# Local attention of a windowed block: maxima over 8x7 queries with two heads side by side, key blocks of nine columns, outputs summed in two banks, band loads in rows of eight heads

## The chip, the cores and the metric

The kernel runs on one core of one Trainium2 chip. Times are device microseconds (us) of one execution; shorter is better. PE is the matmul engine TensorE (PEld its weight loads), DVE is VectorE, ACT ScalarE, POOL GpSimd, SP SyncE; SPq and ACTq are the queues through which SP and ACT issue transfers. SBUF is the on-chip memory of 128 partitions, PSUM the eight accumulator banks (`banks` in the rows).

## The reference, cut to what matters

Two images of 128 channels and 56x56 pixels go through a depthwise convolution, three attentions (over block means, over four selected blocks, over a 7x7 window), a gated sum, a convolutional MLP and a normalization. The change is in the window attention (8 heads of 16 channels, edge padding by 3):

```python
padded = jnp.pad(feat, ((0, 0), (3, 3), (3, 3), (0, 0)), mode='edge')
patches = jnp.stack([padded[:, dy:dy + 56, dx:dx + 56, :] for dy in range(7) for dx in range(7)], axis=3)
q = lin(Q, wq_w[2], wq_b[2]);  k = lin(patches, wk_w[2], wk_b[2]);  v = lin(patches, wv_w[2], wv_b[2])
attn = softmax(einsum('bnhd,bnwhd->bnhw', q, k) * 16 ** -0.5, axis=-1)
y_win = lin(einsum('bnhw,bnwhd->bnhd', attn, v), pj_w[2], pj_b[2])
y = g[..., 0:1] * y_cmp + g[..., 1:2] * y_sel + g[..., 2:3] * y_win + Q
```

## The kernel before, in words

The program has four stretches: convolution and small products (to about 98 us), projection of keys, queries and values of the window attention (`pjobs`, to about 232), the two small attentions (`c_body`, to about 382), the window attention (to about 712), then the MLP.

**Projection.** 42 jobs, 28 of keys and 14 of queries. PE projects (L629), ACT, DVE and POOL split each result into three bf16 parts whose sum is the f32 value (`pk`, a ring of four buffers), and SP stores all three with one DMA to `k_parts` or `q_parts` in DRAM (L370). ACT may refill a buffer only when its store has landed (L875).

**Window attention.** The work is cut in 14 jobs, one for each band of eight image rows of each image. A job's keys are a padded band of 14 rows and 62 columns, stored column by column (`KROWS` = 14). `K` and `Q` hold for each head 96 rows of products of parts (`TERMS`: six pairs of a query part and a key part, 16 rows each), then 30 rows of masks that add a huge negative number to every key outside a query's window, and 2 rows (`SHIFT0`) with the query's negated maximum. `load_band` brings a band two to three jobs ahead; ACT issues it in three groups, each one DMA of keys (L345, 1736-byte rows) and two of queries (L348, 896-byte rows).

A job has 16 steps (`STEPJ`), two for each of 8 strips of 7 columns (`SUBS`, 56 queries). In one step PE issues, in this order:
- A (L732): scores for the maxima of two heads, 112 queries (two strips) against 280 keys, 12 steps ahead of use (`LEAD`); DVE takes the maximum (L1264, `wn`);
- every fourth step S (L739): a transpose of the maxima, after DVE has split them in two bf16 parts (L1270, L1272); DVE copies it (L1277, `nT`) and SP moves it into the shift rows of `Q` (L403);
- scores (L751): keys as the stationary operand, 128 by 56 columns for each of 8 heads, into bank 4 or 5. ACT takes the exponential of the first 98 or 84 partitions (L929, `P`). The 13 key columns of a strip are taken as 7 and 6, one step each (`HCOLS`);
- products with the values (L766), two steps behind: for each head 17 output rows (16 channels and a row of ones, that gives the sum of the exponentials) in a quarter of the partitions, 56 columns, f32, which the trace shows as two passes. The two steps of a strip are summed in bank 6 or 7; ACT copies the strip to `OB` (L943).

After a job's last strip, SP moves the sums to `SR` (L419), DVE turns them into gated reciprocals in three bf16 parts (L1245 to L1255), SP spreads them (L426, `RB`), PE expands them (D, L776), DVE multiplies (L1282, `ON`), PE projects (Y, L782), DVE adds to `X` (L1292). A, S, D and Y share two slots of two PSUM banks in turn (`pa`, `slot_free`): each waits until DVE has read the slot that the second last of them wrote. SP also brings the values `Vw` for each strip and half (L414, 544-byte rows), from a ring of six.

The order on each engine is written out by the step number `q`. Engines wait on semaphores, and each engine runs its own list in order.

## Time and profile before

| | us |
|---|---|
| median of 3 runs (919.23 to 923.59) | 923.09 |
| span of the profiled execution | 922.4 |
| of it: first maxima to first scores of the window attention | 10.9 |
| first scores to last product with the values | 305.7 |
| from there to the last Y | 13.7 |
| PE busy over the whole span | 787.8 |
| DVE busy | 687.8 |
| ACT busy | 371.2 |

The profiled execution's own time is known only by its span. Busy times are unions: matmuls overlap in the array, so a step's cost on PE is read from the distance of two starts, not from the mean duration of an instruction. A line number is that of kernel.py before. PEclk is the granted clock of TensorE, 1.00 for 2.4 GHz and 0.50 for 1.2 GHz.

### The profile page before, as it was taken

The numbers are of one execution on the slowest core, as the hardware profiler recorded it, in microseconds if no ns is written. First come the engines' busy times: TensorE is split into PE (matmuls) and PEld (weight loads), VectorE is DVE, ScalarE is ACT, GpSimd is POOL, SyncE is SP. The second block draws the span as 40 slices with busy tenths as digits, with TensorE's granted clock in tenths as the row PEclk, the third lists the DMA queues.
The fourth block names the chain that finished last, engine by engine and source line by source line (L and its number), as shares of the span: only waits on it lengthen the run. The fifth ranks groups of instructions, "written<-read, shape, count | busy, mean of one in ns | idle before, by whom it ended". The sixth has DMA issues, their size and how long they took to land.

```text
span 922.4 us, 19487 instructions
## 1 busy us (share of the span) xinstructions
PE 787.8 (85%) x7573; PEld 452.1 (49%) x7573; DVE 687.8 (75%) x1442; ACT 371.2 (40%) x721; POOL 175.4 (19%) x236
## 2 busy tenths in 40 slices
PE   4958877776999999799888898888887999999993
PEld 2535433332344444366656666656664454455551
DVE  6976555665889999666777667677784988999971
ACT  2220334443333434134444444444455305445755
POOL 1100233332434444150000000000041034700000
PEclk9966888997689999857999888899999999999998
DMA  5000344554991000036676666677510000000000
GB/s 205 0 1 0 102 138 132 146 150 136 175 172 15 1 1 1 7 90 125 133 143 132 121 125 111 125 146 143 108 44 9 1 0 1 0 1 35 36 35 35
DMA packets 79504, 71.03 MB, mean 77 GB/s; under 512 B 10506, under 2 KB 77878, under 8 KB 78902
## 3 DMA queue, kind: packets, MB, share of 16 engines
q1 hardware_dynamic: 60934, 47.55, 21.4%
q10 hardware_dynamic: 18480, 22.24, 12.2%
q8 instruction: 60, 0.98, 0.5%
q14 instruction: 30, 0.25, 0.1%
HBM read 47.51 MB, written 21.57 MB: 75 GB/s over the span
## 4 chain that ended last, share of the span: by engine, by line
PE 38%; DVE 24%; issue 7%; ACT 4%; DMA 2%; ACTq 1%; SPq 1%; POOL 0%; DVEq 0%
PE banks L827 11%; DVE wn L1264 6%; PE banks L766 5%; PE banks L732 5%; PE banks L751 4%; DVE mx L1198 4%; DVE sm L1211 3%; PE banks L782 3%; DVE AC L1030 2%; DVE ON L1282 2%; DVE sm L1213 1%; DMA RB<-SB 1%; PE banks L716 1%; DVE SEB L1201 1%; ACTq L348 1%
## 5 line engine op out<-in xcount | busy, mean ns | idle before, releaser
L1264 DVE TENSOR_REDUCE wn<-banks 112x2 f32<-112x560 f32 x224 | 162.0, 737 | 53.6 <-PE banks L732 52.6
L929 ACT ACTIVATE P<-banks 98x448 f32<-98x448 f32 x224 | 120.0, 541 | 167.8 <-PE banks L751 133.6
L827 PE MATMUL banks<-FP,PTB 128*128 128x392 f32 x384 | 129.2, 493 | 1.0 <-DVE c L1295 0.9
L1030 DVE SCALAR_TENSOR_TENSOR AC<-XT,vec,AC 128x1540 f32<-128x1540 f32 (+5 forms) x48 | 115.1, 2401 | 1.1
L827 PEld LDWEIGHTS banks<-FP,PTB 128*128 128x128 f32 x384 | 72.8, 190 | 55.5 <-DVE c L1295 1.6
L766 PE MATMUL banks<-P,Vw 84*17 84x56 f32 (+1 forms) x3584 | 95.1, 227 | 2.1 <-issue 1.5
L479 POOL TENSOR_TENSOR SEB<-SEB,rg 112x392 f32<-112x392 f32 x112 | 58.3, 541 | 92.8 <-DVE rg L1218 92.8
L732 PE MATMUL banks<-K,Q 126*112 126x280 bf16 x288 | 71.1, 333 | 4.2 <-DVE wn L1264 3.7
L1127 DVE TENSOR_TENSOR pr<-pf,pk 128x434 f32<-128x434 f32 (+1 forms) x42 | 33.9, 807 | 51.1 <-ACT pk L884 50.3
L908 ACT ACTIVATE SEB<-SEB 112x424 f32<-112x424 f32 x56 | 31.2, 557 | 92.3 <-DVE SEB L1201 92.3
L463 POOL TENSOR_TENSOR pk<-pr,pk 128x434 bf16<-128x434 f32 (+1 forms) x42 | 42.7, 1018 | 127.9 <-DVE pk L1138 127.9
L766 PEld LDWEIGHTS banks<-P,Vw 84*17 84x17 f32 (+1 forms) x3584 | 55.9, 102 | 13.7 <-issue 2.8
L691 PE MATMUL banks<-PTB,VP 106*128 106x448 f32 x112 | 55.8, 587 | 4.8 <-ACT PTB L917 4.8
L751 PE MATMUL banks<-Q,K 128*128 128x56 bf16 x1152 | 56.9, 192 | 1.7 <-ACT P L929 1.7
L671 PE MATMUL banks<-Af,XT 128*112 128x424 f32 x112 | 56.0, 584 | 0.0
L751 PEld LDWEIGHTS banks<-Q,K 128*128 128x128 bf16 x1152 | 49.8, 100 | 9.8 <-issue 2.6
L514 POOL MEMSET FP<- 128x224 f32 x1 | 0.3, 284 | 268.4 <-PE banks L751 268.4
L553 PE MATMUL banks<-X,diag 128*128 128x440 f32 (+3 forms) x90 | 36.4, 569 | 12.6 <-ACT diag L847 12.6
L883 ACT ACTIVATE pf<-banks,vec 128x434 f32<-128x434 f32 x28 | 17.3, 617 | 70.2 <-PE banks L629 49.1
L1198 DVE TENSOR_REDUCE mx<-banks 112x8 f32<-112x392 f32 x112 | 37.1, 373 | 10.4 <-PE banks L672 10.3
L732 PE MATMUL banks<-FP 126*112 126x280 bf16 x160 | 38.7, 331 | 5.0 <-DVE wn L1264 3.2
L732 PEld LDWEIGHTS banks<-K,Q 126*112 126x112 bf16 x288 | 28.8, 140 | 25.5 <-DVE wn L1264 9.7
(225 smaller groups left out, 1294.1 us busy)
## 6 DMA issues: line engine op xcount, KB each, us to landing
k_parts<-pk SPq DMA_DIRECT2D x28, 325.5 KB, 4.0
K<-k_parts ACTq DMA_DIRECT2D x21, 434.0 KB, 5.1
Vw<-v_rows SPq DMA_DIRECT2D x112, 52.1 KB
FP<-k_parts ACTq DMA_DIRECT2D x12, 434.0 KB, 5.0
Vw<-v_rows SPq DMA_DIRECT2D x112, 44.6 KB
q_parts<-pk SPq DMA_DIRECT2D x14, 336.0 KB, 4.3
Q<-q_parts ACTq DMA_DIRECT2D x42, 112.0 KB, 5.3
v_rows<-vst SPq DMA_DIRECT2D x14, 263.5 KB
```

The lines of the kernel that those rows point to most:

```text
L463: g.tensor_tensor(p[:, SLOT[2], 0:cols], pr[n % 3][:, 0:cols], p[:, SLOT[1], 0:cols], ALU.subtract).then_inc(sem("parts_ready"), 1)
L479: g.tensor_tensor(dst, src, by, ALU.mult).then_inc(sem("c_norm"), 1)
L671: mm(s, XT[:, img, ds(t * BAND + c * TILE, TILE)], Af[img][:], start=True, stop=False)
L691: last = mm(bank(4 + img, C, BAND), VP[img][:, j, :], PT[img][:, j, :], start=(j == 0), stop=(j == PAIRS - 1))
L732: last = mm(PS[0:TILE, 2 * slot + e, 0:KROWS * TCOLS], Q[j % BUFS][0:SHIFT0, h, c * TILE:(c + 1) * TILE], K[j % BUFS][0:SHIFT0, h * KBAND ...
L751: last = mm(PS[:, 4 + q % 2, h * SUB:(h + 1) * SUB], K[j % BUFS][:, first:first + 128], Q[j % BUFS][:, h, c * SUB:(c + 1) * SUB], start=Tr ...
L766: last = mm(PS[QUAD * b:QUAD * b + VH, 6 + s % 2, u * SUB:(u + 1) * SUB], Vw[s % VRING][0:HKEYS[half], half, VH * h:VH * (h + 1)], P[p % 4 ...
L827: last = mm(bank(2 + place_in_unit, C, ZPIX), WT[:, dy, part, C * grp:C * (grp + 1)], D[:, part, QROWS * q + dy:QROWS * (q + 1) + dy, :].r ...
L929: a(P[q % 4][0:HKEYS[half], :], PS[0:HKEYS[half], 4 + q % 2, 0:HEADS * SUB], ACT.Exp).then_inc(sem("w_exp"), 1)
L1030: return ve.scalar_tensor_tensor(out=o, in0=src(ro + dy, rn, co + dx, cn), scalar=v(wcol + t), in1=o, op0=ALU.mult, op1=ALU.add)
L1198: ve.tensor_reduce(mx[:, ty, :, :], groups(ps, ty), AX.X, ALU.max).then_inc(sem("c_max"), 1)
L1264: ve.tensor_reduce(wn[tl % 2][:, 2 * hp:2 * hp + 2], src, AX.X, ALU.max, negate=True).then_inc(sem("w_slot_read"), 1)
```

## The change

- **Maxima.** A is done for one strip of 56 queries (64 columns are read, 8 of them of the next strip) against its 182 keys (`SKEYS`), for all 8 heads: even heads write PSUM partitions 0 to 63, odd heads 64 to 127, two pairs to a bank. There are 8 A in a job instead of 16, each with 8 matmuls of 182 columns instead of 2 of 280. One DVE reduction covers 128 partitions with 4 rows of 182. S makes two transposes, and the copy `nT` has 224 columns on 8 partitions.
- **Key blocks.** The 62 padded columns are cut into 7 blocks of 9 (`KW`, the last has 8), without overlap. A block is multiplied with all queries whose window touches it: 72 in the first, 120 in five, 64 in the last (`BQ`). A step takes four heads of one block: 14 steps in a job. The mask's rows follow (`XCLASS`).
- **Outputs.** The products of all seven blocks are summed in banks 6 (heads 0 to 3) and 7 (heads 4 to 7), three steps behind the scores (`PVLAG`); ACT copies 448 columns twice in a job instead of 112 columns eight times.
- **Transfers.** The parts lie in DRAM by channel, band and head, so that the eight heads of a row are contiguous: 13888 bytes of keys, 7168 of queries. A band takes three groups of two DMAs (48, 32 and 16 rows). Values come once for each block (126 rows), 7 DMAs in a job instead of 16, in a ring of eight. The store of the parts is three DMAs instead of one.
- **Order.** A is at 8 of the 14 steps (`MAX_AT`), S at `TURN_AT`, the sums at offset 17 from the job's first step, reciprocals at 21, D at 27 and Y at 30 (before 19, 26, 32 and 35, of steps of the old kind). Queries lie column by column within a band, so L853 and L1292 have other strides.

```diff
+KW = 9
+BLOCKS = -(-PSIDE // KW)
+BX0 = [max(0, KW * b - (WIN - 1)) for b in range(BLOCKS)]
+BQ = [BLOCK * (min(SIDE, KW * b + BCOLS[b]) - BX0[b]) for b in range(BLOCKS)]
+MQ = 64
+SKEYS = KCOLS * KROWS
-TERMS = ((0, 1), (0, 0), (1, 1), (1, 0), (2, 0), (0, 2))
+TRUNS = ((0, 48, 3), (1, 16, 2), (2, 0, 1))
-VRING = 6
+VRING = 8
...
-        STEPJ = 2 * SUBS
+        STEPJ = 2 * BLOCKS
+        PVLAG = 3
+        MAX_AT = (0, 1, 3, 5, 7, 8, 10, 12)
+        TURN_AT = (4, 8, 11, 15)
+        TILE_NEEDED = {0: 0, 2: 1, 6: 2, 8: 3}
+        SUMS_AT, RECIP_AT, PARTS_AT, NORM_AT, Y_AT = 17, 21, 22, 27, 30
...
-            src = k_dram[first:first + 2, :, img, t * KBAND:(t + 1) * KBAND].rearrange("t (d h) n -> (t d) h n", h=HEADS)
-            queue.dma_start(kd[r0:r0 + 2 * DH, :, :], src).then_inc(done, 16)
-            for e in range(2):
-                src = q_dram[SLOT[TERMS[2 * part + e][0]], :, img, t * BAND:(t + 1) * BAND].rearrange("(d h) n -> d h n", h=HEADS)
-                queue.dma_start(Q[j % BUFS][r0 + DH * e:r0 + DH * (e + 1), :, :], src).then_inc(done, 16)
+            qpart, r0, n = TRUNS[part]
+            src = k_dram[0:n, :, img, t].rearrange("t d h n -> d t (h n)")
+            queue.dma_start(K[j % BUFS][r0:r0 + DH * n, 0:HEADS * KBAND], src).then_inc(done, 16)
+            src = q_dram[qpart, :, img, t].rearrange("d h n -> d (h n)")
+            queue.dma_start(QB[j % BUFS][r0:r0 + DH * n, 0:HEADS * BAND], bc(src.unsqueeze(1), [DH, n, HEADS * BAND])).then_inc(done, 16)
...
-                sp.dma_start(dst.rearrange("t c n -> c t n"), pk[n % RING][:, :, 0:cols]).then_inc(sem(f"parts_stored{n % RING}"), 16)
+                for part in range(3):
+                    dst = (k_dram if which == "k" else q_dram)[part, :, m, band, :, off:off + cols]
+                    sp.dma_start(dst, pk[n % RING][:, part, 0:cols]).then_inc(sem(f"parts_stored{n % RING}"), 16)
...
-                        for e in range(2):
-                            h = 2 * hp + e
-                            last = mm(PS[0:TILE, 2 * slot + e, 0:KROWS * TCOLS], Q[j % BUFS][0:SHIFT0, h, c * TILE:(c + 1) * TILE],
-                                      K[j % BUFS][0:SHIFT0, h * KBAND + 14 * c * KROWS:h * KBAND + (14 * c + TCOLS) * KROWS], start=True, stop=True)
+                        for h in range(HEADS):
+                            p, e = divmod(h, 2)
+                            first = h * KBAND + SUBC * c * KROWS
+                            last = mm(PS[MQ * e:MQ * (e + 1), 2 * slot + p // 2, p % 2 * SKEYS:(p % 2 + 1) * SKEYS],
+                                      QB[j % BUFS][0:SHIFT0, h * BAND + c * SUB:h * BAND + c * SUB + MQ], K[j % BUFS][0:SHIFT0, first:first + SKEYS], start=True, stop=True)
...
-                    for h in range(HEADS):
-                        first = h * KBAND + (SUBC * c + HCOLS[0] * half) * KROWS
-                        last = mm(PS[:, 4 + q % 2, h * SUB:(h + 1) * SUB], K[j % BUFS][:, first:first + 128],
-                                  Q[j % BUFS][:, h, c * SUB:(c + 1) * SUB], start=True, stop=True)
+                    for g in range(4):
+                        h = 4 * u + g
+                        first = h * KBAND + KW * b * KROWS
+                        last = mm(PS[:, 4 + q % 2, g * BQ[b]:(g + 1) * BQ[b]], K[j % BUFS][:, first:first + 128],
+                                  Q[j % BUFS][:, h, BLOCK * BX0[b]:BLOCK * BX0[b] + BQ[b]], start=True, stop=True)
...
-                    for h in range(HEADS):
-                        u, b = divmod(h, 4)
-                        last = mm(PS[QUAD * b:QUAD * b + VH, 6 + s % 2, u * SUB:(u + 1) * SUB], Vw[s % VRING][0:HKEYS[half], half, VH * h:VH * (h + 1)],
-                                  P[p % 4][0:HKEYS[half], SUB * h:SUB * (h + 1)], start=(half == 0 and u == 0),
-                                  stop=(half == 1), skip_group_check=True)
+                    if b == 0 and j >= 1:
+                        pe.wait_ge(sem("w_out"), 2 * (j - 1) + u + 1)
+                    for g in range(4):
+                        h = 4 * u + g
+                        last = mm(PS[QUAD * g:QUAD * g + VH, 6 + u, BLOCK * BX0[b]:BLOCK * BX0[b] + BQ[b]], Vw[s % VRING][0:BKEYS[b], VH * h:VH * (h + 1)],
+                                  P[p % 4][0:BKEYS[b], BQ[b] * g:BQ[b] * (g + 1)], start=(b == 0), stop=(b == BLOCKS - 1), skip_group_check=True)
```

On PE, in the middle of a job around D (L776 before, L802 after), this stood in a row before: D, then A, then S, then scores (L751) and products (L766).

```order
L766 MATMUL banks<-P,Vw 17x56 x8
L776 MATMUL banks<-RB,spread 128x448 x2
L732 MATMUL banks<-K,Q 112x280 x2
L739 MATMUL banks<-identb,wnb 16x112
L751 MATMUL banks<-Q,K 128x56 x8
```

In the changed kernel A is L755, S is L763, scores are L777, products L793:

```order
L763 MATMUL banks<-identb,wnb 8x128 x2
L777 MATMUL banks<-Q,K 128x64 x4
L793 MATMUL banks<-P,Vw 17x120 x4
L802 MATMUL banks<-RB,spread 128x448 x2
L755 MATMUL banks<-FP 64x182 x8
L777 MATMUL banks<-FP 128x72 x4
```

S now comes before D, and the second A after D comes two steps later; before, an A and an S stood right behind D.

On ACT, around the first of the three groups of band loads, before (exponential L929, key load L345, query loads L348, copy L943):

```order
L929 ACTIVATE P<-banks 84x448
L345 DMA FP<-k_parts 32x8x868
L348 DMA FP<-q_parts 16x8x448 x2
L929 ACTIVATE P<-banks 98x448
L943 ACTIVATE OB<-banks 128x2x56
```

and now (exponential L955, loads L369 and L371, copy L969):

```order
L955 ACTIVATE P<-banks 112x256 x2
L369 DMA K<-k_parts 48x1x6944
L371 DMA Q<-q_parts 48x1x3584
L955 ACTIVATE P<-banks 126x288 x2
L969 ACTIVATE OB<-banks 128x448
```

Two DMA instructions stand between exponentials instead of three, and the copies of the outputs are two in a job.

On SP, after the load of the sums (L419 before, L441 after), with values L414 and shift rows L403 before:

```order
L419 DMA SR<-OB 64x1x56
L414 DMA Vw<-v_rows 98x1x136
L414 DMA Vw<-v_rows 84x1x136
L403 DMA FP<-nT 2x8x112
L414 DMA Vw<-v_rows 98x1x136
```

and now, with values L436 and shift rows L427:

```order
L441 DMA SR<-OB 64x1x56
L427 DMA FP<-nT 2x8x112
L436 DMA Vw<-v_rows 126x1x136 x2
L427 DMA Q<-nT 2x8x112
L436 DMA Vw<-v_rows 126x1x136
```

The transfer of a tile's shift rows follows the sums directly, and that tile is read by the scores five steps after its S; before it was seven.

## Rows read from the trace of the kernel before

**Rows 1.** The page, busy time of the engines: us (share of span) xinstructions.

```profile
PE 787.8 (85%) x7573; PEld 452.1 (49%) x7573; DVE 687.8 (75%) x1442; ACT 371.2 (40%) x721; POOL 175.4 (19%) x236
```

**Rows 2.** Busy time by stretch: PE, PEld, DVE, ACT, POOL, PEclk, DMA share, GB/s.

```profile
98.00:232.00 134.00, 96.78 (x337) 43.75 (x337) 78.24 (x199) 54.94 (x99) 41.84 (x42) 0.88 0.49 139
381.70:392.60 10.90, 7.63 (x27) 3.64 (x28) 8.73 (x18) 0.00 (x0) 0.00 (x0) 0.60 0.08 20
392.60:424.80 32.20, 31.16 (x495) 22.63 (x494) 20.33 (x38) 12.06 (x28) 13.39 (x8) 0.50 0.37 94
424.80:698.30 273.50, 239.99 (x5435) 170.22 (x5433) 199.50 (x476) 123.59 (x308) 10.97 (x19) 0.94 0.60 120
```

**Rows 3.** Timeline, DVE, the first reciprocal of two jobs that follow each other.

```profile
612.59 0.48 DVE L1245 RECIPROCAL SR<-SR 64x56 f32<-64x56 f32 x1
...
633.32 0.48 DVE L1245 RECIPROCAL SR<-SR 64x56 f32<-64x56 f32 x1
```

**Rows 4.** Timeline, PE, full clock: start, us, what; D, then plain steps, then Y.

```profile
620.61 0.55 PE L776 MATMUL banks<-RB,spread 128*128 128x448 bf16 x2
621.14 0.45 PE L732 MATMUL banks<-K,Q 126*112 126x280 bf16 x2
622.55 0.21 PE L739 MATMUL banks<-identb,wnb 112*16 112x112 bf16 x1 [0.96 <-DVE c L1284]
...
623.33 0.45 PE L732 MATMUL banks<-K,Q 126*112 126x280 bf16 x2
623.61 0.37 PE L751 MATMUL banks<-Q,K 128*128 128x56 bf16 x8
623.91 0.39 PE L766 MATMUL banks<-P,Vw 98*17 98x56 f32 x16
624.23 0.45 PE L732 MATMUL banks<-K,Q 126*112 126x280 bf16 x2
...
625.14 1.77 PE L782 MATMUL banks<-ON,W 128*128 128x448 f32 x4
```

**Rows 5.** Timeline, PE, at half clock: a plain step, then Y.

```profile
556.48 0.58 PE L751 MATMUL banks<-Q,K 128*128 128x56 bf16 x8
...
558.01 0.58 PE L751 MATMUL banks<-Q,K 128*128 128x56 bf16 x8
...
559.03 2.92 PE L782 MATMUL banks<-ON,W 128*128 128x448 f32 x4
```

**Rows 6.** Costliest groups: line, what, xcount | busy us, mean ns | idle before.

```profile
L1264 DVE TENSOR_REDUCE wn<-banks 112x2 f32<-112x560 f32 x224 | 162.0, 737 | 53.6 <-PE banks L732 52.6 <-DVE wnb L1272 0.3
L929 ACT ACTIVATE P<-banks 98x448 f32<-98x448 f32 x112 | 60.8, 543 | 112.9 <-PE banks L751 79.2 <-PE banks L766 18.6 <-issue 14.7
L1198 DVE TENSOR_REDUCE mx<-banks 112x8 f32<-112x392 f32 x56 | 31.6, 565 | 10.4 <-PE banks L672 10.3
L943 ACT ACTIVATE OB<-banks 128x112 f32<-128x112 f32 x112 | 29.0, 259 | 17.7 <-PE banks L766 10.4 <-issue 7.2
```

**Rows 7.** Timeline, a band load issued by ACT, and who waits then.

```profile
613.10 2.10 ACTq L348 DMA_DIRECT2D Q<-q_parts  x2
...
615.99 0.37 PE L751 MATMUL banks<-FP 128*128 128x56 bf16 x8 [0.61 <-ACT P L929]
```

**Rows 8.** Busy time by stretch, columns as in rows 2, around changes of the clock.

```profile
504.00:508.00 4.00, 2.51 (x52) 1.55 (x49) 2.77 (x7) 1.18 (x3) 0.00 (x0) 0.84 0.86 175
508.00:512.00 4.00, 4.00 (x54) 2.91 (x55) 1.82 (x4) 1.30 (x4) 0.00 (x0) 0.50 0.44 87
512.00:516.00 4.00, 3.55 (x40) 1.90 (x39) 1.89 (x5) 0.54 (x1) 0.00 (x0) 0.80 0.18 30
```

**Rows 9.** DMA issues of the page: what, xcount, KB each, us to landing.

```profile
K<-k_parts ACTq DMA_DIRECT2D x21, 434.0 KB, 5.1
```

**Rows 10.** Projection stretch, who waited for whom: us, times, longest.

```profile
ACT pf L883 <- DMA k_parts<-pk: 22.9, 7, 4.2
```

**Rows 11.** The store's issues on SP: ns min/median/max, first and last start in us.

```profile
L370 SPq DMA_DIRECT2D k_parts<-pk x28: 359/360/3862, 98.2 to 183.7; - x28
```

More of the change, by code:

```diff
@@ L49 @@
 SC = PAIRS * KC
-SLOT = (1, 0, 2)
-TERMS = ((0, 1), (0, 0), (1, 1), (1, 0), (2, 0), (0, 2))
+SLOT = (0, 1, 2)
+TRUNS = ((0, 48, 3), (1, 16, 2), (2, 0, 1))
+TERMS = sum(n for _, _, n in TRUNS)
 NGRP = IMAGES * BANDS
-MASK0 = len(TERMS) * DH
+MASK0 = TERMS * DH
 SHIFT0 = 126
@@ L310, in place, with job_at, turned_at @@
+        STEP_RANGE = range(-LEAD, STEPS - STEPJ + Y_AT + 1)
         def place(j):
             return divmod(j, IMAGES)
+        def job_at(q, offset):
+            j, r = divmod(q - offset, STEPJ)
+            return j if r == 0 and 0 <= j < JOBS else None
+        def turned_at(q):
+            found = []
+            for k, at0 in enumerate(TURN_AT):
+                j = job_at(q + LEAD, at0)
+                if j is not None:
+                    found.append(TILES * j + k)
+            return found
@@ new lines, in build @@
+            for k, at0 in enumerate(MAX_AT):
+                if job_at(q + LEAD, at0) is not None:
+                    jobs.append(("A", SUBS * job_at(q + LEAD, at0) + k))
+            jobs += [("S", n) for n in turned_at(q)]
+            if job_at(q, NORM_AT) is not None:
+                jobs.append(("D", job_at(q, NORM_AT)))
+            if job_at(q, Y_AT) is not None:
+                jobs.append(("Y", job_at(q, Y_AT)))
+            for kind, n in jobs:
+                order = len(pa_order)
+                pa_order[kind, n] = order
+                pa.setdefault(q, []).append((kind, n, order % 2, order))
@@ L329, in build @@
+        assert sum(k == "A" for k, n in pa_order) == SUBN
         NQ = IMAGES * QUARTERS
@@ L737, in _ @@
                         slot_free(order)
-                        dst = PS[0:2 * HEADS, 2 * slot, 0:TILE // 2].bitcast(BF16)
-                        tr(dst, wnb[n % 2][:].rearrange("p a h -> p (a h)"), identb[:]).then_inc(sem("w_slot"), 1)
+                        dst = PS[0:HEADS, 2 * slot, 0:128].bitcast(BF16)
+                        for c in range(2):
+                            last = tr(dst[:, 128 * c:128 * (c + 1)], wnb[n % 2][:, c, :, :].rearrange("p a j -> p (a j)"), identb[:])
+                        last.then_inc(sem("w_slot"), 1)
@@ L924, in _ @@
                 if 0 <= q < STEPS:
-                    half = q % 2
+                    b = q % STEPJ // 2
                     act.wait_ge(sem("w_scores"), q + 1)
```

198 lines of the change are left out of this document (91 added, 107 removed).

## The prediction

> **What bounds the kernel now.** I read the page's busy times first: PE is busy 85% of the span, DVE 75% [rows 1]. That is a mean over five stretches, so I go by stretch [rows 2]. The window attention, 305.7 us from first scores to last product, is a third of the time and nearly all that the change touches; its first 32.2 us run at PEclk 0.50, the other 273.5 us at 0.94. Next the job's period, from the same instruction of two neighbouring jobs at full clock: 633.32 - 612.59 = 20.7 us [rows 3]. At a clock of 0.94 the half-clock share is 12%.
>
> What fills 20.7 us? A plain step is 624.23 - 623.33 = 0.90 us, PE running without a hole: A 0.28, scores 0.30, products 0.32 [rows 4]. D takes 0.53 (620.61 to 621.14), an S some 0.17, Y about 1.6 (its row says 1.77, with the end modelled) [rows 4]. Sum: 16 x 0.90 + 0.53 + 4 x 0.17 + 1.6 = 17.2. The remaining 3.5 us are waits. One stands in the rows: the S behind D waits 0.96 us for a slot that DVE holds [rows 4]; another is ACT, which issues loads for 2.10 us, after which PE waits 0.61 us for an exponential, three times a job [rows 7]. DVE's sum for a job is nearly as long: 16 maxima x 0.74 [rows 6] alone are 11.8 us. So PE's work bounds a job, with DVE and ACT close enough to make it wait.
>
> **Pricing the new matmuls.** I take each group of rows 4 apart into columns at 2.4 GHz and a rest. A: 2 x 280 columns are 0.23, rest 0.05. Scores: 8 x 56 = 448 columns are 0.19, rest 0.11. Y: four passes of 448 columns in at most 1.77 us are two clocks for a column of f32 (1.49 us). By that the 16 passes of a products group would take 16 x 56 x 2 / 2.4 = 0.75 us one after another; the row says 0.32. Four heads, each in its own quarter of the partitions, must run side by side: 0.19, rest 0.13.
>
> New products: 8 passes x 120 x 2 / 2.4 / 4 = 0.20, plus 0.13: 0.33. New scores: 4 x 120 columns are 0.20, plus 0.11: 0.31. A step without A is 0.64 (120 columns), 0.48 (72), 0.45 (64): 10 x 0.64 + 2 x 0.48 + 2 x 0.45 = 8.3 us for a job.
>
> New A: 8 x 182 columns are 0.61 if they follow each other, 0.30 if the two heads of a pair run side by side in the two halves. No row shows halves; the quarters of the products are the nearest and do overlap, so I take 0.30, with a rest of 0.13 as between the other groups of unlike width: 0.43. Bounds 0.35 and 0.74. 8 x 0.43 = 3.4 us; before it was 16 x 0.28 = 4.5, so merging saves little on PE here. S makes two transposes: 4 x 0.25 = 1.0. D and Y stay. PE's sum: 8.3 + 3.4 + 1.0 + 0.5 + 1.6 = **14.8 us**, against 17.2.
>
> **DVE and ACT.** 560 elements take 0.737 us and 392 take 0.565 [rows 6], so 728 take 0.737 + 168 x 0.00102 = 0.91; eight are 7.3 instead of 11.8 us. The rest of DVE's job (splits, copies, reciprocals, D and Y) stays: 199.5 us busy [rows 2] in 203 steps or 12.7 jobs are 15.7 a job, less 11.8 leaves 4 to 5. DVE has about 12.5 us. ACT: 448 columns are 0.54 and 112 are 0.26 [rows 6], 0.83 ns a column; ten exponentials of 480 columns (0.57), two of 288 (0.41), two of 256 (0.38) and two copies (0.54) are 8.4 us instead of 10.8. Six DMA issues instead of nine at about 0.6 are another 3.6. Neither passes 14.8.
>
> **Waits of the new job.** The S behind D is gone: after D come one A on the other slot and nearly two steps before D's slot is wanted. This 0.96 us goes at no cost, since DVE's multiplication is hidden behind A, scores and products; with a late D it would be back. Y still has an S behind it that wants its slot: DVE's addition less the A between, 0.7. ACT's loads block less (two instructions), 0.5 in all. New: the shift rows of the fourth tile have five steps between their S and the scores that read them, some 5 us with the A's among them. In this time fall PE's A (0.43), DVE's maximum (0.91) with split and copy (some 0.6), SP's issue (up to 1.05, half of the 2.10 us that ACT takes for two [rows 7]) and the landing. The landing of a small transfer is in no row. Nearest is the 5.1 us of 434 KB under load [rows 9], which would end 3.1 us late; at the other end there is no wait. This one carries 3.5 KB, so I take 0.7, near the low end. It would hold the scores, and behind them on PE the products, all A and thus DVE. Sundries 0.6. Sum 2.5 (bounds 1.2 and 5): **17.3 us** for a job at full clock.
>
> At half clock a plain step is (558.01 - 556.48) = 1.53 us and Y 2.9 [rows 5]. The same arithmetic at 1.2 GHz gives 0.74 for A, 1.08, 0.76 and 0.71 for the other steps, 24.7 + 1.5 = 26.2 us for a job, and 1.54 us for a mean step before the first D.
>
> **The clock.** The stretch begins at half clock, and in its first 32.2 us PE is busy 31.16 us and stays at 0.50 [rows 2]. Later it falls after thin PE work (2.51 us busy of 4, around D) and comes back in the 4 us in which a Y runs [rows 8]. The new steps fill PE about as the old ones do: 0.40 of 0.64 us are columns without A, 0.70 of 1.07 with it, before 0.61 of 0.90. I keep 12% for the middle, 1 / (0.88 / 17.3 + 0.12 / 26.2) = 18.0 us for a job; for the start I take 25 steps at half clock, between the 21 of before and the 28 that reach the first Y.
>
> "TensorE: Matmul & The Clock Gate" of the Trainium skill (Part 1) says that activity releases the throttle. Taken alone this would end the slow start almost at once; the row of 32.2 us disagrees, and the sum goes by the row.
>
> **The sum.** Start: 25 x 1.54 = 38.5 us. The other 171 steps are 12.2 jobs x 18.0 = 220. Together 258.5 instead of 305.7: **-47**. Lead: 12 A's took 10.9 us [rows 2], DVE bound; now 7 A's of 0.91 and their splits are 8.4: -2.5. After the last product the chain of sums, D and Y is the same: 0. Projection: the store becomes three DMAs of a third each. ACT already waits 22.9 us in 7 cases for landed key stores [rows 10]; two more issues of 0.36 us [rows 11] delay the last third by 0.7 us; 7 times that is 5, and -2 if thirds land sooner; I take +2. The first copies (L853) and Y's addition only change strides, 0. Total -47.5: 922.4 - 47.5 = 874.9 for the profiled execution; the median is 0.7 above its span, so 876.
>
> "DMA: Bandwidth & Descriptors" of the Trainium skill (Specifications) asks for at least 512 bytes a row for full rate. By that rows of 1736 and 896 bytes were long enough and longer ones gain nothing; I give them no gain either, since no row shows PE waiting for a band load.
>
> **Rivals.**
> 1. *Halves don't overlap.* Each A costs 0.74 instead of 0.43: 8 x 0.31 = 2.5 us a job, 14 jobs 35 us: 911. For it: no row shows halves. Against: quarters overlap.
> 2. *Small transfers become the bound.* With shorter steps, shift rows, sums or reciprocals arrive late behind rows of 13888 bytes: 2.5 us more for a job, 35 us: 911. For it: SP has less distance in front of it (five steps instead of seven; D ten steps after the sums instead of thirteen). Against: fewer and larger transfers on both queues.
> 3. *The clock.* If PE ran at full clock throughout, its busy steps having ended the slow start: 14 x 17.3 = 242 instead of 258.5, 860. (The rule of "TensorE: Matmul & The Clock Gate" in the Trainium skill, above, would bring this about.) If instead the holes that remain, being a larger share of a shorter job, pull the clock down, and Y alone brings it back, the gain goes. With 43 us at the start, the other 12 jobs may take (305.7 - 43) / 12 = 21.9 us, and a job takes that when 52% of its work is done at half clock (0.48 x 17.3 + 0.52 x 26.2 = 21.9). From there the change is slower. Three quarters of the work would be 24.0 a job, 43 + 288 = 331, 948; all of it 14 x 26.2 = 367, 984. For it: the slow start, in which busy steps did not help. Against: 88% of the middle was at full clock.
> 4. *PE was not the bound.* If waits of DVE and transfers set the job and the change only moves them: 20.7 us stays, 922. Against: the sums of PE, DVE and ACT all fall.
>
> **How the numbers follow.** My forecast, 855 to 897: 0.64. Rival 1 0.08, rival 2 0.12, clock at full 0.04, clock low and slower 0.08, no change 0.04. The range of 8 in 10 takes in rivals 1 and 2 and waits of 1.2 us a job (12.2 x 1.3 = 16 below): 857 to 914. A measurement of this kernel tells 0.5%, 4.6 us, from no change. Faster by more: 0.64 + 0.08 + 0.12 + 0.04 = 0.88; within: 0.04; slower: 0.08.
>
> **What would show it.** Right: period of a job 17 to 18 us at full clock; A's group 0.43 us from start to next start; maxima 0.91 us; no wait of S behind D. Wrong: A's group near 0.74; PE waiting before scores for shift rows or before D for `RB`; PEclk well below 0.9 in the middle; projection stretch longer than 134 us [rows 2] by more than 6.

## The result and the profile after

The changed kernel takes 886.82 us (median; 886.04 to 890.88) where the kernel before takes 921.16 (911.09 to 923.59). The ratio is 0.969, 95% interval 0.964 to 0.973: faster by 3.1%, inside the stated range of 857 to 914, 11 us above the forecast of 876. Its profiled execution has a span of 884.3 us; line numbers below are those of the changed kernel, or of the experiment named.

The page of the changed kernel: busy times, then the chain of work that ended last. They answer to [rows 1].

```profile
PE 739.2 (84%) x5053; PEld 384.9 (44%) x5053; DVE 636.1 (72%) x1330; ACT 354.8 (40%) x609; POOL 175.5 (20%) x239
...
PE banks L853 12%; DMA Q<-nT 5%; PE banks L793 5%; PE banks L777 5%; PE banks L755 4%; DVE mx L1224 4%; DVE sm L1237 3%; PE banks L808 3%; DMA FP<-nT 3%; DVE AC L1056 2%; DVE wn L1291 2%; DVE X L1319 2%; DVE sm L1239 2%; PE banks L739 1%; DVE SEB L1227 1%
```

PE has 49 us less work. New on the chain are `Q<-nT` and `FP<-nT` (the same kind of transfer; one of the three buffers has another name in the profile), 8% of the span: the 3.5 KB of shift rows that the scores of a query tile need. The stretches, columns as in [rows 2]: lead, the first two jobs or so, the rest up to the last scores.

```profile
386.60:396.70 10.10, 6.15 (x70) 3.81 (x70) 7.57 (x16) 0.00 (x0) 0.00 (x0) 0.64 0.07 16
396.70:424.80 28.10, 23.66 (x394) 14.35 (x393) 21.06 (x41) 13.22 (x26) 13.41 (x8) 0.89 0.59 148
424.80:657.10 232.30, 195.21 (x2940) 108.36 (x2939) 148.52 (x362) 98.18 (x195) 11.02 (x19) 0.88 0.58 115
```

The start runs at PEclk 0.89, where before it was 0.50 for 32.2 us; the rest runs at 0.88, where it was 0.94. From first scores to last product it is 262.6 us, forecast 258.5. Within it the first 25 steps took 28.6 us instead of the 38.5 forecast, and the other 171 took 234 instead of 220: two errors of opposite sign. A job takes 20.3 us on average from the third to the twelfth (forecast 18.0; before 22.2, and 20.4 to 20.8 where no half-clock spell fell in it).

PE's waits in the attention: us in total, times, longest.

```profile
PE banks L777 <- DMA Q<-nT: 20.1, 8, 2.9
PE banks L763 <- DVE c L1321: 9.3, 11, 0.8
PE banks L777 <- DMA FP<-nT: 8.0, 4, 3.3
```

The scores (L777) wait once a job for shift rows, 28.1 us in 12 waits. One of them in the timeline (start, us, engine, line, what, [idle before <- releaser]; the rows of DVE's maxima and of ACT's exponentials are left out):

```profile
553.87 0.27 PE L763 MATMUL banks<-identb,wnb 128*8 128x128 bf16 x2 [0.84 <-DVE c L1321]
...
554.50 0.56 ACTq L369 DMA_DIRECT2D K<-k_parts  x1
...
554.89 0.26 DVE L1304 COPY nT<-banks 8x224 bf16<-8x224 bf16 x1
...
555.09 0.61 ACTq L371 DMA_DIRECT2D Q<-q_parts  x1
555.18 0.68 SPq L427 DMA_DIRECT2D Q<-nT  x1
...
557.15 0.51 PE L755 MATMUL banks<-FP 126*64 126x182 bf16 x8
...
557.59 0.38 PE L777 MATMUL banks<-Q,K 128*128 128x120 bf16 x4
...
557.91 0.40 PE L793 MATMUL banks<-P,Vw 126*17 126x120 f32 x8
...
560.43 0.58 PE L777 MATMUL banks<-Q,K 128*128 128x120 bf16 x4 [2.13 <-DMA Q<-nT]
```

Read it as a chain. At 553.87 the fourth tile's transposes run; they had waited 0.84 us behind Y. DVE copies them, and SP issues their transfer at 555.18. It lands 5.2 us later, at 560.43, and everything behind the scores on PE has stood still since 558.3. At 554.50, 0.7 us ahead, ACT had issued a group of the next band's loads. Both go through the core's 16 DMA engines, which are 95% busy from 556 to 560. The packets of the shift rows (224 B each, the only ones of that size then) began at 558.80, 3.6 us after the issue, when the group's were nearly through. Around it the clock:

```profile
552.00:556.00 4.00, 3.16 (x52) 1.68 (x54) 2.65 (x8) 0.76 (x2) 0.00 (x0) 1.00 0.59 134
556.00:560.00 4.00, 2.23 (x43) 1.26 (x42) 3.40 (x11) 1.98 (x4) 0.00 (x0) 1.00 0.95 195
560.00:564.00 4.00, 3.56 (x40) 1.94 (x40) 0.92 (x1) 1.14 (x2) 0.00 (x0) 0.51 0.73 92
564.00:568.00 4.00, 4.00 (x58) 2.26 (x60) 2.26 (x5) 1.52 (x3) 0.00 (x0) 0.64 0.14 16
568.00:572.00 4.00, 4.00 (x64) 2.23 (x65) 3.30 (x8) 2.57 (x6) 0.00 (x0) 1.00 0.79 186
```

The 4 us with the wait have PE at 2.23 us busy; in the next the granted clock is 0.51, and the first of these windows that is wholly at 1.00 again is the one from 568. So a wait of 2 us costs a second time, in steps at half clock. It is no single case: after 425 us PE waited for shift rows ten times for 2.0 to 3.3 us, and the trace has ten half-clock spells there (3.4 or 6.8 us), each beginning during such a wait or within 2 us of its end.

The parts that stand outside: the projection took 127.2 us from first to last matmul before and takes 133.7 now. The combination stretch behind it (the two small attentions) is 5.8 us shorter and the set-up ahead of it 4.2 longer; no line of either is changed but L853, whose copies are L879 now (e4 below), and both hold half-clock spells of differing length in every profile.

### The profile page after: what moved, and what is told of

Its sections match the earlier page's. It is cut to its first block, busy times and chain, and to the rows that moved or that the text cites. A ratio compares the mean times of both kernels' runs of the same rounds, so it can differ in the third digit from the quotient of the medians.

```text
span 884.3 us, 14113 instructions
## 1 busy us (share of the span) xinstructions
PE 739.2 (84%) x5053; PEld 384.9 (44%) x5053; DVE 636.1 (72%) x1330; ACT 354.8 (40%) x609; POOL 175.5 (20%) x239
## 4 chain that ended last, share of the span: by engine, by line
PE 37%; DVE 20%; DMA 8%; issue 5%; ACT 4%; SPq 0%; POOL 0%; DVEq 0%; ACTq 0%
PE banks L853 12%; DMA Q<-nT 5%; PE banks L793 5%; PE banks L777 5%; PE banks L755 4%; DVE mx L1224 4%; DVE sm L1237 3%; PE banks L808 3%; DMA FP<-nT 3%; DVE AC L1056 2%; DVE wn L1291 2%; DVE X L1319 2%; DVE sm L1239 2%; PE banks L739 1%; DVE SEB L1227 1%
## 5 line engine op out<-in xcount | busy, mean ns | idle before, releaser
L955 ACT ACTIVATE P<-banks 126x480 f32<-126x480 f32 (+2 forms) x196 | 100.7, 520 | 164.5 <-PE banks L777 153.7
L1291 DVE TENSOR_REDUCE wn<-banks 128x4 f32<-128x728 f32 x112 | 101.7, 911 | 67.4 <-PE banks L755 66.3
L853 PE MATMUL banks<-FP,PTB 128*128 128x392 f32 x384 | 129.2, 493 | 1.4 <-DVE c L1322 1.2
L853 PEld LDWEIGHTS banks<-FP,PTB 128*128 128x128 f32 x384 | 72.8, 190 | 55.8 <-DVE c L1322 1.9
L793 PE MATMUL banks<-P,Vw 126*17 126x120 f32 (+2 forms) x1568 | 79.4, 279 | 0.0
L777 PE MATMUL banks<-Q,K 128*128 128x120 bf16 (+2 forms) x504 | 49.9, 228 | 20.8 <-DMA Q<-nT 20.1
L714 PE MATMUL banks<-PTB,VP 106*128 106x448 f32 x112 | 52.7, 558 | 5.1 <-ACT PTB L943 5.1
L777 PEld LDWEIGHTS banks<-Q,K 128*128 128x128 bf16 x504 | 28.8, 104 | 42.6 <-DMA Q<-nT 22.5
L755 PE MATMUL banks<-K,Q 126*64 126x182 bf16 x576 | 40.7, 269 | 0.0
L1227 DVE TENSOR_TENSOR SEB<-banks,mx 112x392 f32<-112x392 f32 x112 | 37.1, 373 | 1.9
L674 PE MATMUL banks<-xc,gl 128*4 128x448 f32 x28 | 16.1, 662 | 25.8 <-ACT sq L916 25.8
L1056 DVE SCALAR_TENSOR_TENSOR FP<-X,vec,FP 128x3025 f32<-128x3025 f32 (+5 forms) x16 | 36.1, 2259 | 0.6
```

The costliest lines, as they stand in the source:

```text
L714: last = mm(bank(4 + img, C, BAND), VP[img][:, j, :], PT[img][:, j, :], start=(j == 0), stop=(j == PAIRS - 1))
L755: last = mm(PS[MQ * e:MQ * (e + 1), 2 * slot + p // 2, p % 2 * SKEYS:(p % 2 + 1) * SKEYS], QB[j % BUFS][0:SHIFT0, h * BAND + c * SUB:h * B ...
L777: last = mm(PS[:, 4 + q % 2, g * BQ[b]:(g + 1) * BQ[b]], K[j % BUFS][:, first:first + 128], Q[j % BUFS][:, h, BLOCK * BX0[b]:BLOCK * BX0[b ...
L793: last = mm(PS[QUAD * g:QUAD * g + VH, 6 + u, BLOCK * BX0[b]:BLOCK * BX0[b] + BQ[b]], Vw[s % VRING][0:BKEYS[b], VH * h:VH * (h + 1)], P[p ...
L853: last = mm(bank(2 + place_in_unit, C, ZPIX), WT[:, dy, part, C * grp:C * (grp + 1)], D[:, part, QROWS * q + dy:QROWS * (q + 1) + dy, :].r ...
L955: a(P[q % 4][0:BKEYS[b], 0:4 * BQ[b]], PS[0:BKEYS[b], 4 + q % 2, 0:4 * BQ[b]], ACT.Exp).then_inc(sem("w_exp"), 1)
```

## The experiments

Theory Q (queue): small transfers on SP's queue land late behind the bytes of band loads on ACT's, and this wait, with the half-clock steps after it, is what holds a job at 20 us. Rival P (place): the transposes simply stand too close to their scores. Others asked after the halves, the clock, the strides and the stores. Each ratio is to runs of the kernel before on the same chip (medians 916 to 928 us), so two rows that differ by less than about 1% are not told apart; "job" is the mean distance from one job to the next, third to twelfth, and waits are sums in us.

| run | us | ratio to before (95%) | job, us | PE's largest waits for transfers |
|---|---|---|---|---|
| changed kernel | 886.8 | 0.969 (0.964 to 0.973) | 20.3 | shift rows 28.1 |
| e1 | 930.8 | 1.008 (1.003 to 1.012) | 24.3 | RB 63.8 |
| e2 | 850.3 | 0.926 (0.919 to 0.932) | 16.3 | RB 8.6 |
| e6 | 843.2 | 0.912 (0.906 to 0.918) | 15.9 | RB 0.9 |
| e10 | 883.9 | 0.954 (0.946 to 0.961) | 19.8 | shift rows 24.0 |
| e8 | 865.8 | 0.936 (0.928 to 0.943) | 17.4 | RB 3.2 |
| e12 | 906.4 | 0.990 (0.985 to 0.994) | 21.2 | RB 2.3; DVE for sums 42.8 |
| e13 | 840.1 | 0.920 (0.914 to 0.925) | 15.5 | RB 2.3 |
| e3 | 881.5 | 0.957 (0.953 to 0.961) | 20.0 | shift rows 25.4 |
| e4 | 882.9 | 0.961 (0.956 to 0.966) | 19.6 | shift rows 21.6 |
| e5 (of before) | 922.7 | 0.997 (0.992 to 1.001) | 21.6 | RB 0.2 |
| e9 (of before) | 909.6 | 0.984 (0.975 to 0.992) | 21.4 | RB 1.2 |
| e11 | 855.9 | 0.922 (0.914 to 0.930) | 16.8 | RB 8.8, shift rows 2.3 |

**No band loads.** The later jobs compute on bands that already lie in the buffers (PE's wait for a band is lowered to match), so the output is wrong and only the time is of use.

```diff
-                    if j is not None and j + BUFS < JOBS:
+                    if j is not None and j + BUFS < BUFS:
                         load_band(act, j + BUFS, part)
```

> The changed kernel without the band loads of jobs 3 to 13: these jobs compute on the bands that lie in the buffers, so the output is not the reference's. ACT issues no loads and the DMA queues carry none in the attention. Queue theory (the shift rows of the fourth tile land late because their transfer stands behind a band load): PE's wait for shift rows before the scores of step 8 (28.1 us in 12 waits) goes entirely, with it the half-clock spells that begin there; period 20 falls to 15.5 to 16.5 us, stage 215 to 230, whole 835 to 855. Rival (five steps are too short for the chain of split, transposes, copy and transfer even on idle queues): each wait stays at 1 us or more, period 18 or more, whole over 860.

843.17 us, inside the theory's range. The same place in its timeline, then a window of 180 us:

```profile
507.79 0.27 PE L763 MATMUL banks<-identb,wnb 128*8 128x128 bf16 x2 [0.84 <-DVE c L1321]
...
509.10 0.68 SPq L427 DMA_DIRECT2D Q<-nT  x1
...
512.03 0.38 PE L777 MATMUL banks<-Q,K 128*128 128x120 bf16 x4
```

```profile
420.00:600.00 180.00, 167.32 (x2799) 96.16 (x2797) 140.82 (x349) 92.90 (x184) 3.17 (x6) 1.00 0.15 36
```

The places of the instructions are the same, the distance is the same (1.3 us from transposes to issue, 2.9 from issue to scores), and there is no wait. The packets begin 1.32 us after the issue (median of ten jobs) where the changed kernel has 3.74, and the transfer is marked complete 0.4 us after its last packet, behind loads 1.0 to 2.0. No half-clock spell is left in these 180 us, nor in the rest of the attention but its start. Theory Q holds, and P falls as a cause: five steps are enough on idle queues. The 20.3 us of a job are 15.9 without loads, 2.3 of wait, and a remainder of 2.1, most of it the half-clock steps: e2 below has the loads but few waits and takes 16.3.

**Other places for the loads.** Groups 0, 6, 10 steps after a job's end, later 0, 2, 8:

```diff
-                for part, off in enumerate((0, 4, 8)):
+                for part, off in enumerate((0, 6, 10)):
```

> The changed kernel, with the second and third group of a band's loads issued by ACT two steps later (6 and 10 steps behind the first instead of 4 and 8). In the changed kernel PE waits once a job, 2.0 to 3.3 us, before the scores of the fourth tile, for its shift rows (Q<-nT), whose transfer was issued right behind the second group of loads. Theory (queue): the small transfer stands behind the bytes of the band load; with the load behind it, it lands about 2 us earlier, the wait falls to 0 to 0.7 us, and with it the half-clock spells that begin at that wait: 886 falls to 840 to 865 us. Rival (distance): the transfer takes that long anyway and only the five steps between S and its use are too few: 2 to 3 us of wait stay, 883 to 890 us. A new wait for the reciprocals (RB), behind the third group, would be a cost of up to 1 us a job.

> The changed kernel with the second group of band loads two steps earlier (loads 0, 2, 8 steps after the end of a job instead of 0, 4, 8); it was issued 0.7 us before the shift rows of the fourth tile. Queue theory: most of that group's 5.5 us has passed when the shift rows are issued, PE's wait before the scores of step 8 (2.0 to 3.3 us) falls under 1.5, a job gets 1.5 to 3 us shorter, whole 850 to 868; the wait for RB, which came when a group stood ahead of it, stays absent, since the third group keeps its place. Rival (the load is in the way wherever it stands, some other transfer of the job then waits: two groups in four steps are a single block of 10 us): the wait stays over 2 us, 875 to 900.

e1 missed by at least 66 us: 930.79. The wait for shift rows is gone, as said, but its place was taken. PE's waits in the attention, then one in the timeline:

```profile
PE banks L802 <- DMA RB<-SB: 63.8, 12, 6.2
```

```profile
575.82 0.93 PE L802 MATMUL banks<-RB,spread 128*128 128x448 bf16 x2 [6.00 <-DMA RB<-SB]
```

D (L802) needs `RB`, which SP sends in three small transfers 5 steps ahead of it. One load group now goes out 3 steps before them, another at the same time:

```profile
565.22 1.94 SPq L448 DMA_DIRECT2D RB<-SB  x3
...
565.62 0.32 ACTq L369 DMA_DIRECT2D FP<-k_parts  x1
```

The packets of these three transfers run from 569.10 to 574.41, between those of both groups. So load bytes issued just behind a small transfer hold it up too. It is 5.3 us of wait a job, where I had allowed 1, and 7 to 14 us at half clock around it. e10, 883.94, ends on the rival's side:

```profile
PE banks L777 <- DMA Q<-nT: 17.2, 8, 4.6
...
PE banks L777 <- DMA FP<-nT: 6.8, 4, 3.4
```

24.0 instead of 28.1 us in 12 waits. Two groups within two steps are one block of bytes; the gather of the sums, issued at 535.38 in one job, had its first packets at 540.24, and the shift rows stand behind it in SP's own queue. What counts is all the load bytes around a small transfer's issue, not the last group's distance.

**Earlier transposes.** The fourth tile's maxima and transposes two steps sooner, the loads where they were:

```diff
-        MAX_AT = (0, 1, 3, 5, 7, 8, 10, 12)
-        TURN_AT = (4, 8, 11, 15)
+        MAX_AT = (0, 1, 3, 4, 6, 7, 9, 10)
+        TURN_AT = (4, 8, 11, 13)
```

> The changed kernel, with the maxima of the later tiles and the fourth S earlier (MAX_AT 0 1 3 4 6 7 9 10, TURN_AT 4 8 11 13): the fourth tile's shift rows now have seven steps, and their transfer is issued before the second group of loads. Both queue and distance expect the wait of 2.6 us a job to go. What it tells: whether the half-clock spell of each job goes with the wait (then 840 to 865 us) or stays because Y and the denser maxima leave other holes (then 860 to 875 us).

850.25 us (848.63 to 859.37), the fastest kernel here that does all of the work. Shift rows still take long (first packet a median 3.5 us after the issue for this tile, 5.2 for the third, the packets counted off in the order of issue), but nobody waits: seven steps lie between. PE's largest wait, and the window of the middle:

```profile
PE banks L802 <- DMA RB<-SB: 8.6, 8, 2.3
```

```profile
428.00:619.00 191.00, 175.99 (x2911) 101.96 (x2909) 147.95 (x358) 96.94 (x193) 10.14 (x18) 0.99 0.68 140
```

PEclk is 0.99 with the same loads in flight (DMA share 0.68, more than the 0.58 of the changed kernel). So transfers in flight did not lower the clock; in the changed kernel it fell where PE had waited. The edit moves the transfer both further from its use and ahead of a load group, so e2 alone does not tell Q from P; e6 does.

**What is left to gain from there.** D and Y one step later (`NORM_AT, Y_AT = 28, 31` for `27, 30`); loads at 0, 3, 6; and no loads:

> As the kernel with earlier transposes (850.25 us), with D one step later (28 instead of 27 steps into the job) and Y one later (31 instead of 30). There PE waited for the reciprocals (RB) 8 times, 8.6 us in all, up to 2.3. Theory (RB's three transfers take some 5 us and any step of distance is worth its length): the wait falls below 3 us in all, a job gets 0.4 to 0.8 us shorter, 840 to 847. Rival (D and Y then meet other slots: the S of the first tile behind Y waits more, gains and losses cancel): 848 to 855.

> The kernel with earlier transposes (850.25 us), with the band loads of a job 0, 3 and 6 steps after its end instead of 0, 4 and 8. There the third group is issued two steps before the reciprocals' transfers (RB), and PE waited 8.6 us for them in 8 waits. Theory (a small transfer waits for the load bytes that are under way when it is issued): the bytes are through two steps sooner, RB's wait falls under 4 us in all, and the shift rows of the fourth tile, which have six steps there, still arrive in time: 843 to 849. Rival (denser loads delay the gather of the sums and the shift rows more than they free RB, as with loads at 0, 2, 8): PE waits for shift rows again, 852 to 870.

> The kernel with earlier transposes, without the band loads of jobs 3 to 13 (these jobs compute on the bands in the buffers, so the output is not the reference's). It is the floor that the loads leave to any placement. Theory: RB's wait goes, a job takes 15.4 to 15.6 us as the undisturbed ones do now (15.5 at best), stage 212 to 218, whole 832 to 842, and no more than 5 us under the changed kernel without reloads (843.17 us). Rival (the waits on DVE's slots set the job in the earlier order): periods stay at 16 or over, 845 to 850.

e8, 865.76 us: RB's wait fell as said, to 3.2 us, and the whole got 15 us longer, past even the rival. Two other waits grew. D and Y share PSUM slots with A and S, and one step later they meet them in another order:

```profile
PE banks L763 <- DVE wn L1291: 13.9, 24, 1.7
PE banks L755 <- DVE c L1311: 7.8, 11, 0.7
```

These two are 12.2 us more than in e2, and two more half-clock spells fall in the middle. That these waits explain all of the 15 us is not shown. e12, 906.40 us, is past both ranges, by half of the rival's mechanism. PE waits 49.1 us for maxima; the cause shows on DVE, its waits, then one in the timeline:

```profile
DVE SR L1271 <- DMA SR<-OB: 42.8, 12, 5.3
```

```profile
512.36 0.49 DVE L1271 RECIPROCAL SR<-SR 64x56 f32<-64x56 f32 x1 [3.13 <-DMA SR<-OB]
...
513.94 1.72 DVE L1291 TENSOR_REDUCE wn<-banks 128x4 f32<-128x728 f32 x2
514.99 0.37 PE L763 MATMUL banks<-identb,wnb 128*8 128x128 bf16 x2 [3.29 <-DVE wn L1291]
```

The gather of the sums lands late: one load group was issued 1.8 us before it, another 2.4 us after it, and its last packets come 7.1 us after its issue; DVE stands at the reciprocal, and two maxima queue behind it. After shift rows and RB it is the third small transfer of a job to be caught. e13, 840.13, inside the theory's range: the floor, 15.5 us a job. So e2 loses about 10 us to loads by the medians (7.8 by the attention stages of the two profiles; the ratios' intervals overlap), the changed kernel 44 against e6.

**The halves.** A's heads in the order 0, 2, 4, 6, 1, 3, 5, 7, so that all matmuls of one half stand together:

```diff
-                        for h in range(HEADS):
+                        for h in (0, 2, 4, 6, 1, 3, 5, 7):
```

> The changed kernel, with the eight matmuls of an A in the order of heads 0 2 4 6 1 3 5 7, so that neighbours write the same half of the partitions. If pairs overlap only as neighbours in different halves (theory), an A goes from 0.44 us to about 0.74 us at full clock, 8 x 0.3 = 2.4 us a job, partly hidden in the wait for shift rows: 895 to 920 us. If the halves did not overlap, or the order did not matter, nothing changes: 886 us.

881.45 us, no slower. Its timeline:

```profile
583.13 0.52 PE L755 MATMUL banks<-K,Q 126*64 126x182 bf16 x8
583.57 0.30 PE L777 MATMUL banks<-Q,K 128*128 128x72 bf16 x4
```

0.44 us again. 8 x 182 columns are 0.61 us at 2.4 GHz in a row, so the halves overlap in both orders. The single starts tell how (us from 583.1):

```
changed order of heads: .026 .039 | .129 .142 | .210 .220 | .288 .299
```

They come in pairs 10 to 13 ns apart, though four of one half were issued first. In the changed kernel the two of a pair are at most 3 ns apart. The trace does not name the half, but 182 columns at 2.4 GHz are 76 ns, so two that start 13 ns apart can hardly be in the same one. Nor do the times fit the order of issue: with four of one half first and the other half starting no earlier than the fourth of them, the last would start at least 6 x 76 = 456 ns after the first; it starts 273 ns after it. A half, it seems, works off its own matmuls and does not wait for the other's. The run was meant to bring rival 1's case about and could not; rival 1 falls by the 0.44 us itself. "TensorE: Matmul & The Clock Gate" of the Trainium skill (Part 2) says that matmuls stay in program order; by these starts that can hold only within a half.

**The start's clock.** In the kernel before, each matmul of A twice during the first two jobs:

```diff
-                        for e in range(2):
+                        for e in (0, 1, 0, 1) if n < 2 * STEPJ else (0, 1):
```

> The kernel before, whose attention starts with 41 us at half clock, with each matmul of A issued twice (the same values written again) in the first two jobs, to see whether the thinner streaming of the old steps kept the clock low. The changed kernel had only 10 us there. Theory (more streamed columns end the slow start): the half-clock spell at the start shrinks to 10 to 20 us; step 25 is reached no later than before (38 us after step 0) although PE has 0.23 to 0.47 us more work for each A, whole 905 to 925. Rival (the spell has nothing to do with how much A streams): the spell stays at 38 us or more and the added work makes the whole 928 to 936.

909.63 us: more work, less time, by two runs (1.6%, interval 0.8 to 2.5%). The end of the lead, and the stretch that answers to the slow start of [rows 2]:

```profile
384.00:392.00 8.00, 5.66 (x38) 3.86 (x37) 6.53 (x15) 0.00 (x0) 0.00 (x0) 1.00 0.11 28
392.00:424.00 32.00, 29.41 (x689) 23.38 (x686) 24.05 (x49) 15.21 (x37) 13.41 (x8) 1.00 0.49 119
```

PEclk 1.00 where it was 0.50, with PE's busy time no higher (29.41 of 32 us; before 31.16 of 32.2). The first 25 steps took 31.4 us instead of 38.1. In the kernel before the clock fell in the lead, at 383.9 us, and stayed low for 41 us, with PE busy nearly all the time. In e9 it did not fall in the lead at all. So doubled A's kept the slow spell away here; the run does not show what would end one. That PE's busy time alone does not end one is shown by the two kernels themselves: in the changed kernel the spell began in the lead too, at 389.4, and ended after 10.2 us, with PE busy 7.75 of 10 us (390 to 400). What else it takes stays open.

The size of the effect is not settled either: it is one profile and two times, e5 leaves this stage unchanged and has two spells of 20.5 and 17.1 us, and after 425 us e9 has 20 us at half clock where the kernel before has 34, which belongs to no change of code. The same edit on e2 (first 12 A's), seven of them in the lead:

> The kernel with earlier transposes (850.25 us), with each matmul of A issued twice (the same values) in the first 12 A's, seven of which stand in the lead, where DVE's maxima set the pace. In the kernel before, doubling A removed the half-clock spell at the start. Theory (more streamed columns lift the clock early): no half-clock spell of over 7 us after the first scores, 13.7 and 6.8 us at half clock fall by 10 or more, which is 3 to 5 us of time, against 5 added groups outside the lead at 0.4 to 0.6 us: 846 to 850. Rival (the changed kernel's start has its spell from something else, the thin lead for one): the spell stays and the added work shows, 851 to 855.

855.9 us. The start of e11:

```profile
397.00:430.00 33.00, 25.96 (x439) 15.71 (x440) 26.00 (x45) 14.13 (x27) 13.35 (x8) 0.89 0.53 125
```

e2 has 0.80 there (395.5 to 428). The half-clock time before 433 us falls from 20.5 to 13.6 us, less than the 10 expected, and there are the added groups and a new wait of 2.1 us: nothing gained, and the time is just past the rival's range.

**Strides.** The copies L879 and Y's addition L1319, written so that they walk along image rows; the side in query order (for Y both things read) then steps by 32 B:

```diff
-   ...[:, m, PAD + BLOCK * b:PAD + BLOCK * (b + 1), PAD:PAD + SIDE].rearrange("p r c -> p c r")
-   ...rearrange("p (c r) -> p c r", r=BLOCK)
+   ...[:, m, PAD + BLOCK * b:PAD + BLOCK * (b + 1), PAD:PAD + SIDE]
+   ...rearrange("p (c r) -> p r c", r=BLOCK)
```

> The changed kernel, with the copies into query order (ACT, 14 at the start) and Y's addition (DVE) walking along image rows: the operand in image order is read or written contiguously and the other one with a stride of 32 bytes; before it was contiguous on one side with a stride of 248 or 224 bytes on the other. Theory (any stride over a few elements halves the rate): the copies stay near 1.03 us and the addition near 0.98 us, time 884 to 888 us. Rival (only wide strides cost): 0.58 us and 0.62 us as in the kernel before, 14 x 0.44 = 6 us less at the start, of which 4 were on the path, and 0.36 us a job in front of S: 875 to 882 us.

882.92 us, between the two ranges; the durations decide. Costliest groups, ACT in the set-up and DVE in the attention, of the changed kernel and then of e4:

```profile
L879 ACT ACTIVATE XT<-FP 128x448 f32<-128x448 f32 x14 | 13.2, 1025 | 1.5 <-DVE c L1068 1.5
...
L1319 DVE TENSOR_TENSOR X<-banks,XT 128x448 f32<-128x448 f32 x12 | 11.8, 985 | 10.3 <-PE banks L808 10.3
```

```profile
L879 ACT ACTIVATE XT<-FP 128x448 f32<-128x448 f32 x14 | 11.8, 1025 | 2.4 <-DVE c L1068 2.4
...
L1319 DVE TENSOR_TENSOR X<-banks,XT 128x448 f32<-128x448 f32 x13 | 12.4, 955 | 13.1 <-PE banks L808 13.1
```

Before they took 582 and 625 ns. "Only strides, 0" was wrong: 448 elements cost 0.44 us more on ACT and 0.36 on DVE, and it makes little difference (none on ACT, 3% on DVE) which side has the stride or whether it is 248, 224 or 32 B. "SBUF — State Buffer" of the Trainium skill (Specifications) says that a stride beyond a line of 16 bytes pays; both strides are beyond it, and the rows agree. Little of it reaches the end: 14 x 0.44 = 6.2 us lie in ACT's set-up, where the projection begins at 89.9 to 94.8 us in the kernels with the slow copies and at 90.3 to 92.5 in those with the old ones; Y's 0.36 us make the S behind it wait 0.84 instead of the 0.7 forecast.

**The stores.** In the kernel before, each store as three DMAs of one part, as in the change, in the old layout:

```diff
-                dst = (k_dram if which == "k" else q_dram)[:, :, m, at0:at0 + cols]
-                sp.dma_start(dst.rearrange("t c n -> c t n"), pk[n % RING][:, :, 0:cols])...
+                for part in range(3):
+                    dst = (k_dram if which == "k" else q_dram)[part, :, m, at0:at0 + cols]
+                    sp.dma_start(dst, pk[n % RING][:, part, 0:cols])...
```

> The kernel before with one part of the change alone: each store of projected parts is issued as three DMAs instead of one, in the old layout (rows of 392 to 448 elements stay as they were). The projection stretch was 127.2 us before (90.3 to 217.5) and 133.7 after. Theory (the three stores delay the reuse of the staging buffers, as forecast at +2 with bounds -2 and +6): the stretch becomes 130 to 134 us, the whole 924 to 929. Rival (the layout in rows of eight heads is what costs): the stretch stays at 127 to 128 and the time at 921 to 924.

922.67 us, ratio 0.997: no difference that can be told, and inside the rival's range. Its projection takes 129.4 us, between the two expectations. Two profiles with the old stores have 127.2 and 128.9 (before, e9), the kernels with the new layout 132.4 to 134.2. Three DMAs instead of one explain at most 2 of some 5 us. The rest must come from the rows of eight heads or from something that goes with them; no run separates it, and it stays open.

## Why the prediction was right, and where not

**PE's prices held.** A's group 0.44 us (557.15 to 557.59; forecast 0.43), scores 0.32 (557.59 to 557.91; 0.31), the maxima 911 ns on DVE (0.91), S 0.21 (0.25). With loads and their waits away, a job is 15.9 us, against 16.6 in the forecast without its 0.7 for the shift rows. The sum of PE's groups by start distances, with an overlap taken from the quarters of the products, was the right method for the halves.

**The S behind D** no longer waits, and the S behind Y does, 0.84 us, as forecast.

**The wait for shift rows** was the mis-sized term, and the one sign of being wrong that came in full: 0.7 us in the sum, bounds 0 to 3.1, measured 28.1 / 12 = 2.3. I said that no row showed a small transfer's landing and took a value near the low end because it carries only 3.5 KB. Size was the wrong guide: on idle queues its packets begin after 1.3 us, behind a load after 3.7, and the 5.2 us to landing of this 3.5 KB are near the 5.1 of the 434 KB in [rows 9]. The row to take was the neighbour in time. The trace of the kernel before would have told as much: there, too, first packets of shift rows come late, a median 3.1, 1.4, 2.9 and 2.3 us after the issue for the four tiles of a job, and seven steps hid it (PE waited 0.9 us in all for small transfers, and only for `RB`). That the fourth tile's grew from 2.3 to 3.7 may be the larger load groups or their new places; no run separates these. "DMA: Bandwidth & Descriptors" of the Trainium skill (on rings and completion order) says that a DMA engine takes turns between queues in whole packets and that the mark of completion waits for the earlier writes of that engine, of all its queues. The trace agrees with both in kind: late first packets, and 1.2 us between the last packet (559.21) and PE's start, where on idle queues (e6) the mark comes 0.4 us behind the last packet. It was rival 2, at some 1.6 us a job above the term instead of 2.5.

**The clock in the middle.** I kept 12% at half clock since the new steps fill PE as the old ones did. It was 23% (54 of 232 us): each wait of 2 us or more had a spell of 3.4 or 6.8 us with it. The step that failed is that the wait and the clock were summed apart: the share at half clock was carried over from the old kernel, although the sum itself brought in a new wait.

**The clock at the start** was wrong the other way: 25 steps in 28.6 us instead of 38.5, since only 6.3 us of them ran at half clock (the end of a spell that began in the lead, and one of 3.4 us). I had read the 32.2 us of [rows 2] as a property of the stage's start; it hung on the old steps. In the ten kernels with new steps of the table beside the changed one the first 25 take 26.2 to 34.5 us, before and in e5 38.1 and 37.4, so 28.6 is one draw of several. The rule that activity releases the throttle ("TensorE: Matmul & The Clock Gate" of the Trainium skill, Part 1), which I set aside by that row, came nearer for the new steps; it does not tell the old case apart.

**Together:** 9.9 us gained at the start and 14 lost in the middle leave the stage 4.1 over the forecast. The projection is 6.5 longer (forecast 2), the lead 10.1 instead of 8.4, and the combination 5.8 shorter and the set-up 4.2 longer where I had 0. That the total came within 11 us owes something to luck: errors of opposite sign cancelled. Rival 4 ("20.7 us stays") looked right by the period alone, 20.3; e6 and e2 show that it is not the same 20.7: before, PE's own work was 17.2 of it; now a job takes 15.9 where the loads are away, and the waits for transfers are new.

## What to carry to other kernels

A small transfer can land as late as the large ones around it: price it by the large transfer that is under way when it is issued, look also for one that is issued just after it (e1, e12), and give it that many steps of distance. Moving the large one can just pick another victim: here the same loads in three other places caught RB (e1), the gather and shift rows (e10) and the gather (e12), while two steps more for the one that waited gave 4%. Where TensorE's clock can fall, count each of its waits with the half-clock steps behind it, here nearly as much again.

## What the runs showed of the hardware

- Matmuls into different column halves of the array overlap whatever the order of issue: a group of eight takes 0.44 us in both orders, where 8 x 182 columns in a row are 0.61; they start in pairs at most 3 ns apart when alternating, 10 to 13 ns when four of one half come first (changed kernel, e3).
- The granted clock did not follow PE's busy time at the start: 0.50 at 31.16 us busy of 32.2 (before), 1.00 at 29.41 of 32 (e9). Issuing A's matmuls twice in the first two jobs went with a time 1.6% shorter (0.8 to 2.5%, two runs).
- The 3.5 KB of the fourth tile's shift rows had their first packet 1.32 us after the issue on idle queues (e6) and 3.74 behind band loads (changed kernel), and were marked complete 0.4 us after the last packet against 1.0 to 2.0.
- A stride of 32 B cost as much as one of 248 B, on the read or the write side: 1.025 us against 0.582 without it for 448 f32 on ACT (e4, changed kernel, kernel before).
